# A three-layer GNN kernel on one core: the order of VectorE's work at the end of the rounds, the softmax bound's place, and when two edge tables are loaded

## Time and profile before

| | |
|---|---|
| median of 3 runs | 2980.59 us (2978.1 to 2980.78) |
| the profiled execution | 2978.72 us, of which the span of the profile is 2976.6 us |
| busy: TensorE matmul, VectorE, GpSimd, ScalarE | 2220.9, 2084.0, 1784.8, 632.3 us |
| granted TensorE clock, mean | 0.743 |

### The profile page before, as it was taken

The page is one execution under the profiler, slowest core; times in us unless marked ns, Lnnn a source line. Parts: engine busy times, 40 slices in busy tenths (PEclk is TensorE's granted clock), DMA queues, the critical chain, the costliest instruction groups (busy, mean ns, idle before and its releaser), DMA issues. The chain is left out here.

```text
span 2976.6 us, 64648 instructions
## 1 busy us (share of the span) xinstructions
PE 2220.9 (75%) x13922; PEld 1706.0 (57%) x13923; DVE 2084.0 (70%) x7853; ACT 632.3 (21%) x1180; POOL 1784.8 (60%) x1866
## 2 busy tenths in 40 slices
PE   0288988889898898885799557667677676676748
PEld 0155555555555555555799446656666565566637
DVE  6477777777777777746466557777777777777755
ACT  0323322233322233231000111111111111111100
POOL 0077777777777777730001167777777777777722
PEclk6599999999999999995899555555555555555558
DMA  1144554545545454542000133333333333333330
GB/s 42 51 127 130 143 141 129 142 128 142 140 134 142 127 142 132 141 92 58 20 1 2 35 74 83 80 82 81 81 81 83 80 82 81 82 81 81 81 42 12
DMA packets 425510, 268.62 MB, mean 90 GB/s; under 512 B 334069, under 2 KB 375908, under 8 KB 425444
## 3 DMA queue, kind: packets, MB, share of 16 engines
q0 software_dynamic: 71040, 176.52, 23.5%
q1 hardware_dynamic: 284418, 49.42, 8.7%
q10 hardware_dynamic: 69986, 41.88, 4.6%
HBM read 231.16 MB, written 15.97 MB: 83 GB/s over the span
## 5 line engine op out<-in xcount | busy, mean ns | idle before, releaser
L906 POOL DMA_INDIRECT edges_rows<-table,edges_idx x888 | 863.7, 973 | 294.7 <-issue 231.4
L2073 POOL DMA_INDIRECT all_arena<-table_kv,edges_idx x888 | 855.5, 963 | 276.5 <-issue 256.7
L2265 PE MATMUL edges_acc<-edges_values,edges_into 128*128 128x136 f32 x1776 | 511.6, 461 | 261.1 <-DVE edges_values L2153 244.7
L2265 PEld LDWEIGHTS edges_acc<-edges_values,edges_into 128*128 128x128 f32 x1776 | 416.6, 328 | 308.6 <-DVE edges_values L2153 295.0
L1062 PE MATMUL edges_radial_ps<-edges_rows,edges_into_w 128*128 x1776 | 460.9, 396 | 91.6 <-SPq L916 73.2
L975 DVE TENSOR_SCALAR edges_cell<-edges_ramp,edges_strip_key,first_key 128x400 bf16<-128x400 f16 x1184 | 451.3, 381 | 0.0
L1062 PEld LDWEIGHTS edges_radial_ps<-edges_rows,edges_into_w 128*128 128x128 f32 x1776 | 319.8, 190 | 215.9 <-issue 175.4
L2118 DVE TENSOR_SCALAR edges_ahead<-edges_nodes,edges_starts,edges_dst_f 128x128 bf16<-128x128 f32 x894 | 262.4, 359 | 172.7 <-issue 172.7
L974 DVE TENSOR_SCALAR edges_low<-edges_places,first_src_low 128x128 bf16<-128x128 bf16 x1184 | 330.6, 279 | 0.0
L2199 ACT COPY edges_into_t<-edges_t_ps 128x384 bf16<-128x384 bf16 x298 | 142.6, 479 | 874.4 <-PE edges_t_ps L2233 868.6
L1057 PE MATMUL edges_cells_ps<-edges_cell,edges_low 128*128 128x400 bf16 x1184 | 251.4, 335 | 36.2 <-DVE edges_cell L975 29.9
(11 more groups left out here) (344 smaller groups left out, 2555.8 us busy)
## 6 DMA issues: line engine op xcount, KB each, us to landing
edges_values<-in_edge_attr SPq DMA_DIRECT2D x888, 32.0 KB
all_arena<-all_arena ACTq DMA_DIRECT2D x50, 400.0 KB
edges_rows<-table,edges_idx POOLq DMA_INDIRECT x888
all_arena<-table_kv,edges_idx POOLq DMA_INDIRECT x888
edges_attr<-in_edge_attr ACTq DMA_DIRECT2D x51, 256.0 KB
edges_bias<-bias_kept SPq DMA_DIRECT2D x296, 12.0 KB
bias_kept<-edges_bias_out ACTq DMA_DIRECT2D x52, 64.0 KB
table<-all_arena SPq DMA_DIRECT2D x1, 3250.0 KB, 11.4
```

The costliest lines, as they stand in the source:

```text
L906: pool.indirect_dma_start(rows[:, n, :], None, table0, bass.IndirectOffsetOnAxis(ap=idx[:, n:n + 1], axis=0)).then_inc(s_rows[g], 16)
L2073: pool.indirect_dma_start(rows[:, n, :], None, table_kv, bass.IndirectOffsetOnAxis(ap=idx[:, n:n + 1], axis=0)).then_inc(s_rows[g], 16)
L2265: last = nc.tensor.matmul(acc[:, 0:2 * F + H2], into[:, h, j, :], values[:, h, j, :], start=False, stop=True, skip_group_check=True)
```

## The change

1. VectorE goes through the tail in an order of its own, `late`: fc0, fc1, fc2, kvq0, fc3, kvq1, fc4, kvq2, kvq3, kvq4. TensorE and ScalarE keep `tail`.
2. The bound is computed inside the rounds' program. VectorE takes the largest values (`tops`) in kvq4 between the sums of squares and the split, and does the rest (`bound_on_vector`) at the end of its program; GpSimd's two operations (`bound_on_gpsimd`) follow its last layer norm. The program behind the If is gone; its computation is repeated in the If's body, which isn't run here.
3. SyncE loads the two edge tables in the rounds, after the weights and the bias, into a part of `arena` (`near`) that is free then; VectorE and SyncE of the rounds wait for them. The attention loads nothing first and waits for no tables; its ring of gathered rows moves up in `arena` behind them.

```diff
@@ rounds, before the programs
+            near = Borrowed(nc, "edge_tables", flat, COUNTS)
+            edge_src, edge_dst = near.sb("src_i", [P, TT], I32), near.sb("dst_f", [P, TT])
...
+                late = [("fc", 0), ("fc", 1)]
+                for i in range(2, GR):
+                    late += [("fc", i), ("kvq", i - 2)]
+                late += [("kvq", GR - 2), ("kvq", GR - 1)]
+
+                def bound_on_gpsimd(pool, n):
+
+                    pool.wait_ge(s_top, n)
+                    pool.partition_all_reduce(top_all[:, :], top[:, :], P, RMAX).then_inc(s_all, 1)
+                    pool.wait_ge(s_bound, n)
+                    pool.tensor_tensor(bound[:, :], bound[:, :], half[:, :], ALU.pow).then_inc(s_root, 1)
+
+                def tops(dve, n):
+
+                    dve.tensor_reduce(top[:, 0:2 * H2], norms[:, :, :].rearrange("p w h -> p h w"), AX, ALU.max)
+                    dve.tensor_reduce(top[:, 2 * H2:3 * H2], most[:, :].rearrange("p (j h) -> p h j", h=H2), AX, ALU.max).then_inc(s_top, 1)
+
+                def bound_on_vector(step, dve, n):
+
+                    dve.wait_ge(s_all, n)
+                    dve.tensor_tensor(bound[:, :], top_all[:, 0:H2], top_all[:, H2:2 * H2], ALU.mult).then_inc(s_bound, 1)
+                    dve.wait_ge(s_root, n)
+                    step(dve.tensor_tensor(bound[:, :], bound[:, :], top_all[:, 2 * H2:3 * H2], ALU.add))
+                    step(dve.tensor_tensor(bound[:, :], bound[:, :], b2[:, :], ALU.add))
+                    step(dve.tensor_tensor(lift[:, :], b2[:, :], bound[:, :], ALU.subtract))
@@ rounds, SyncE
                         sp.dma_start(b2[:, :], a["L2_gnn_be2"].partition_broadcast(P)).then_inc(s_ld, 16)
+                        sp.dma_start(edge_src, src_kept).then_inc(s_x, 16)
+                        sp.dma_start(edge_dst, dst_kept).then_inc(s_x, 16)
...
-                        sp.wait_ge(s_x, 16)
+                        sp.wait_ge(s_x, 48)
@@ rounds, GpSimd
                         for e in range(LR + GR):
                             rstd_group(pool, st, e, s_var, s_rstd)
+                        bound_on_gpsimd(pool, 1)
@@ rounds, VectorE
-                        dve.wait_ge(s_x, 16)
-                        for of, g in tail:
+                        dve.wait_ge(s_x, 48)
+                        for of, g in late:
...
                                 step(dve.tensor_reduce(group(norms, g), cat[:, :, :].rearrange("p u (h d) -> p u h d", d=DK), AX, ALU.add))
+                                if g == GR - 1:
+                                    tops(dve, 1)
                                 split_group(step, dve, group4(q3, g), tmp[:, :, :], kvq[:, g % 2, :, 0:F]).then_inc(s_split, 1)
                                 dve.wait_ge(s_split, g + 1)
+                        bound_on_vector(step, dve, 1)
@@ behind the If and its barrier
-                with nc.Block() as block:
...
@@ attention
-                    src_i = ph.sb("src_i", [P, TT], I32)
-                    dst_f = ph.sb("dst_f", [P, TT])
+                    src_i, dst_f = edge_src, edge_dst
...
-                    rows = Borrowed(nc, tag + "_ring", flat, COUNTS).sb("rows", [P, 4 * G, 2 * F])
+                    rows = Borrowed(nc, tag + "_ring", flat, near.at).sb("rows", [P, 4 * G, 2 * F])
...
-                            sp.dma_start(src_i[:, :], src_kept).then_inc(s_ld, 16)
-                            sp.dma_start(dst_f[:, :], dst_kept).then_inc(s_ld, 16)
+                            if clamped:
+                                sp.dma_start(src_i, src_kept).then_inc(s_ld, 16)
+                                sp.dma_start(dst_f, dst_kept).then_inc(s_ld, 16)
...
-                            dve.wait_ge(s_ld, 32)
+                            if clamped:
+                                dve.wait_ge(s_ld, 32)
```

More of the change, by code:

```diff
@@ L1747, in build @@
                 s_kv_st = [ph.sem(f"s_kvq_stored{i}") for i in range(2)]
+                s_top, s_all, s_bound, s_root = (ph.sem(n) for n in ("s_top", "s_top_all", "s_bound", "s_root"))
                 GR = NW // U
@@ L1979, in _ @@
                                 step(dve.tensor_reduce(group(norms, g), cat[:, :, :].rearrange("p u (h d) -> p u h d", d=DK), AX, ALU.add))
+                                if g == GR - 1:
+                                    tops(dve, 1)
                                 split_group(step, dve, group4(q3, g), tmp[:, :, :], kvq[:, g % 2, :, 0:F]).then_inc(s_split, 1)
                                 dve.wait_ge(s_split, g + 1)
-                s_top, s_all, s_bound, s_root = (ph.sem(n) for n in ("s_top", "s_top_all", "s_bound", "s_root"))
-                s_ch2 = ph.sem("s_step2")
+                        bound_on_vector(step, dve, 1)
                 banks.__exit__(None, None, None)
@@ L1989, in build, with _ @@
                     slow_rounds(q3, norms)
+                    s_again = ph.sem("s_tables_again")
+                    with nc.Block() as block:
+                        @block.sync
+                        def _(sp):
+                            sp.dma_start(edge_src, src_kept).then_inc(s_again, 16)
+                            sp.dma_start(edge_dst, dst_kept).then_inc(s_again, 16)
+                            sp.wait_ge(s_again, 32)
+                    s_ch2 = ph.sem("s_step2")
+                    with nc.Block() as block:
+                        @block.gpsimd
+                        def _(pool):
+                            bound_on_gpsimd(pool, 2)
+                        @block.vector
+                        def _(dve):
+                            tops(dve, 2)
+                            bound_on_vector(Chain(dve, s_ch2), dve, 2)
                     nc.all_engine_barrier()
```

## The result

The changed kernel takes 2970.96 us (median of 10 runs, 2966.88 to 2976.66) against 2980.56 (10 runs, 2978.1 to 2988.3): ratio 0.9967, 95% interval 0.9959 to 0.9976, so 7.2 to 12.2 us faster, 9.8 by the ratio. Forecast were 2969.1 and 11.5 us. The profiled execution took 2970.35 us.

What follows compares the result with a forecast made beforehand. Attention was taken as bound by GpSimd's gathers, so the serial path to the first gather counted: 7.6 us up to the attention's start plus 3.9 from the tables, 11.5 us off 2980.6, giving 2969.1; range 2965.5 to 2974.3.

Steps and rivals of the forecast that it cites:

- the main case: Whole kernel: everything goes as told, gain 11.3 to 13.2 us; chance 0.65.
- The order: VectorE's tail of the rounds: the new order starts the last kvq 0.18 us earlier, ends nothing and 0.78.
- The first code load is hidden: Ahead of GpSimd's reduction: load runs under VectorE's kvq2 to kvq4 and costs nothing; without that cover 5.3 us return.
- the first stage's row: Profile row of the first stage: configuration at 3.7, input ready at 32.5, reduction 0.27 us later; evidence for hiding.
- The second load is bare: Between GpSimd's reduction and power: loading back starts when the reduction ends, is not hidden and takes 7.07 us.
- Barriers and jump: Behind the bound: the same barrier and jump, 5.30 us, then the phase's barrier, half of 1.05; attention starts at 1712.39.
- Tables: Attention's start: VectorE's wait of 3.9 us for the tables goes; loading them in the rounds costs nothing.
- what is late next: Attention's start once the table wait is gone: VectorE's own register work, about 1 us, which stays in the sum.
- take nothing: Behind the jump into the attention: a sequencer stall counted as zero, with 2.5 us kept for the range.
- Rival 2: Attention's start: a stall replaces the removed waits, 2.5 us or so less gain, 2971.6; chance 0.14.
- Not slower: Attention's gathers keep their pace; the rival, lost pace with the ring moved, meant net 14.9 us slower, 2995.5; chance 0.03.
- the first linear's cover: Start of the rounds: VectorE's 7.41 us idle for TensorE covers the early table loads, so they cost nothing.

Runs made afterwards that it cites:

- load put late: Changed kernel plus one GpSimd memset waiting for VectorE's tops ahead of the reduction, so the pool configuration is issued after the tops: 2978.41 us, ratio 0.9990.
- tables alone: Kernel before, changed only by loading the edge tables in the rounds: 2980.46 us, ratio 0.9995.

## Why the prediction was right, step by step

The time came inside the stated range, and each station up to the first iota within 0.2 us of its forecast. But the gain of 9.8 us lies below the main case, 11.3 to 13.2: one term was missing from it.

- *The order* was worth 0.18 us in the sum; the profiles show 0.1 to 0.3, hardly clear of the spread between profiles, and no time shows it.
- *The first code load is hidden.* Right: 10.4 us of cover, reduction 0.14 us behind its input. The run with the load put late gives the price, 6 us, so it is shown and not only read from the first stage's row; without cover the bound came 5.5 to 5.7 us later. The Trainium skill (GPSIMD Engine Reference, 2.1 Instruction dispatch), read as "the first call pays", would have cost 5 us here; its figure of about 6 us fits the 5.75 measured, its place of charging doesn't.
- *The second load is bare.* Right: 7.1 us from 1699.4 to 1706.52, as in the earlier trace rows. Taking the switch away took it away.
- *Barriers and jump.* 5.83 us were forecast from the bound to the attention's start; 5.74, 5.90 and 5.90 in three profiles.
- *Tables.* The index copies come within 1.5 us of the attention's start, as said. The mis-sized term is what is late next. The prediction had VectorE's register work, about 1 us, and "take nothing" for a stall of a sequencer behind the jump. The stall is there, on GpSimd: from bound to first gather 8.34 us were forecast, and the three profiles have 9.07, 10.42 and 10.51, so 0.7 to 2.2 us more. Rival 2 named the kind, a price up to 2.5 and the sign, GpSimd idle on "issue" at the attention's start. It gave this a chance of 0.14 beside the main case, where it belonged into the sum with 1.7, the mean of the three profiles. With it the sum is 9.8 us, as the ratio gives; that they agree to a tenth is luck, with an interval of 7.2 to 12.2. In the kernel before, no row shows the stall. That the table wait covered it is read from the run with the tables alone, where the stall stands bare and the first gather gains only 1.5 us.
- *Not slower.* The gather's pace is unchanged (mean 964 ns against 963), and the first linear's cover held to 0.1 us.

## What to carry to other kernels

A GpSimd operation that the compiled program puts behind a `MODIFY_POOL_CONFIG`, as here `partition_all_reduce`, costs its switch from that instruction on, some 6 us there and 7 back (6.9 to 7.5 in eleven profiles). So put such an operation behind a wait that is long anyway, or do without it: for 24 columns two small TensorE steps and three of VectorE were enough. Before you count a removed wait as won, ask what else was standing under it: an engine that sat idle for data may have had a stall of its own that no row shows. When the part of a program that you didn't touch differs by more than the change is worth, measure from the last common point of the trace.

## What the runs showed of the hardware that wasn't expected

- GpSimd's sequencer stalls on its first pass into the attention's program after an If was jumped over, even with a program of 16 us in between (tables alone). Between index copy and first gather 0.8 to 2.0 us of it are bare in the changed kernel and 2.4 with the tables alone; its length differs between runs of the same program, its place with the instructions' position, and in the one profile without the jump it is gone. The Trainium skill (Runtime: NRT & Kernel Launch, Instruction fetch mechanics) says that a taken branch breaks sequential prefetch. That fits all of this, but no row shows the fetch itself, so the cause is argued, not shown.
- The flag and the jump over the If cost 4.3 to 4.5 us beside the barrier (5.74 to 5.90 against 1.41 us from bound to iota). Most of it lies between the branch and the next instruction, in the first profile of the changed kernel 3.3 to 3.8 us on GpSimd, VectorE and SyncE, and 0.42 on ScalarE. Why ScalarE is spared no run here shows.
- Stages ahead of everything that the variants touch differ by up to 10.8 us between the twelve profiles, but by only 1.1 us between the three of one and the same program (rounds' start at 1437.12, 1437.49 and 1438.18). Times of one program still scatter by 10 us. How much of the difference is chance and how much the program's layout is open.
